# One tile step of a macaron transformer kernel: reordered output path, one 17-column power, one sine product per q or k

## The reference, cut to what matters

```python
for l in range(2):                              # the stack, run twice in the kernel
    q, k, v = split(shift_token(x) @ wqkv[l])   # 8 heads of 64
    q, k = l2norm(q) * q_scale, l2norm(k) * k_scale
    q, k = rotary_xpos(q, k)                    # q * cos * s + rotate_half(q) * sin * s, k with 1 / s
    o = local_attention(q * 8, k, v)            # window 64, looks one window back
    x = x + o @ wo
    h = layernorm(shift_token(x)) * g + b
    a, g = split(h @ w1 + b1)
    x = x + (a * gelu(g)) @ w2 + b2
```

## Time and profile before

| | |
|---|---|
| median of 3 runs | 1783.23 us (1782.45 to 1784.5) |
| the profiled execution | 1786.46 us, its span 1784.7 us |
| PE busy | 1515.6 us, 85% |
| DVE busy | 1358.0 us, 76% |
| ACT busy | 1139.9 us, 64% |
| POOL busy | 1095.8 us, 61% |
| mean granted TensorE clock | 0.969 of full speed |

### The profile page before, as it was taken

One profiled execution on the slowest core, in us unless ns is written; L12 is line 12 of the kernel. 1 busy time (PEld: TensorE's weight loads), 2 busy tenths in 40 slices (PEclk: granted clock), 3 DMA queues, 4 the chain that ended last, 5 costly groups with the idle time before them and its releaser, 6 DMA issues.

```text
span 1784.7 us, 44020 instructions
## 1 busy us (share of the span) xinstructions
PE 1515.6 (85%) x15864; PEld 1233.3 (69%) x15864; DVE 1358.0 (76%) x3516; ACT 1139.9 (64%) x2364; POOL 1095.8 (61%) x1106
## 2 busy tenths in 40 slices
PE   1789999978999899977888889989998889999974
PEld 1577777766777777755666667777776777777763
DVE  6687878768787978767776479787977687979772
ACT  1576767667686767634455467676766576767671
POOL 3676868577585858623333278585857485858560
PEclk9899999989999999988999999999999999999996
DMA  8231212132221222113100132121223221212113
GB/s 284 50 122 43 57 41 62 48 95 50 68 51 48 51 71 51 40 29 122 36 25 21 46 96 54 45 54 45 63 57 87 59 60 44 54 44 54 45 28 119
DMA packets 183670, 112.46 MB, mean 63 GB/s; under 512 B 86720, under 2 KB 164128, under 8 KB 182944
## 3 DMA queue, kind: packets, MB, share of 16 engines
q1 hardware_dynamic: 183456, 109.65, 23.5%
HBM read 43.41 MB, written 23.42 MB: 37 GB/s over the span
## 4 chain that ended last, share of the span: by engine, by line
PE 50%; DVE 26%; ACT 9%; issue 7%; SPq 3%; DMA 2%; POOL 1%; DVEq 0%; ACTq 0%; POOLq 0%
PE QK L389 9%; PE TO L639 8%; PE QK L639 5%; PE TO L706 5%; DVE rope_c L1154 5%; DVE rope_s L1159 4%; DVE o_n L1179 4%; DVE top L1098 3%; PE SC L680 3%; ACT probs L1303 3%; PE TO L389 3%; PE TO L752 3%; DVE h2n L1166 3%; PE TO L808 2%; PE VB L808 2%
## 5 line engine op out<-in xcount | busy, mean ns | idle before, releaser
L1303 ACT ACTIVATE probs<-SC,shift,qgain 128x128 f32<-128x128 f32 x1024 | 390.6, 481 | 101.9 <-DVE shift L1106 101.6
L1481 POOL TENSOR_TENSOR ve<-mv,epsilon 128x1 f32<-128x1 f32 x128 | 24.5, 192 | 392.8 <-DVE mv L1145 392.8
L389 PE MATMUL QK<-w_qkv,hT 128*128 128x512 f32 x768 | 220.7, 424 | 25.5 <-DMA w_qkv<-qkv_d 12.0
L1154 DVE TENSOR_TENSOR rope_c<-QK,rope 128x512 f32<-128x512 f32 x256 | 175.7, 686 | 80.5 <-PE QK L389 78.1
L1494 POOL TENSOR_TENSOR rnorm<-clip,mhalf 128x8 f32<-128x8 f32 x128 | 211.1, 1649 | 12.4 <-DVE clip L1115 12.2
L1503 POOL TENSOR_TENSOR qgain<-clip,mhalf 128x8 f32<-128x8 f32 x128 | 209.5, 1637 | 0.0
L639 PE MATMUL TO<-ident,probs 128*128 128x128 f32 x1280 | 189.9, 276 | 12.0 <-ACT probs L1303 11.1
L1098 DVE TENSOR_REDUCE top<-SC 128x4 f32<-128x512 f32 x256 | 174.8, 683 | 31.1 <-PE SC L680 30.9
L1297 ACT ACTIVATE v_own<-VB 128x512 f32<-128x512 f32 x128 | 76.5, 598 | 189.2 <-PE VB L389 189.2
L1159 DVE TENSOR_TENSOR rope_s<-QK,rope 128x256 f32<-128x256 f32 x512 | 191.0, 415 | 0.0
L639 PEld LDWEIGHTS TO<-ident,probs 128*128 128x128 f32 x1280 | 153.8, 142 | 45.0 <-issue 24.8
(11 more groups left out here) (174 smaller groups left out, 3745.0 us busy)
## 6 DMA issues: line engine op xcount, KB each, us to landing
v_prev<-v_own SPq DMA_DIRECT2D x256, 130.0 KB, 2.3
x_att<-stream SPq DMA_DIRECT2D x128, 64.0 KB, 2.2
h<-stream SPq DMA_DIRECT2D x256, 32.0 KB, 1.9
stream<-x_new SPq DMA_DIRECT2D x32, 256.0 KB
w_qkv<-qkv_d SPq DMA_DIRECT2D x3, 1536.0 KB, 7.5
h<-x_mid SPq DMA_DIRECT2D x128, 32.0 KB
h<-x_mid SPq DMA_DIRECT2D x128, 31.8 KB
rope<-rope_d SPq DMA_DIRECT2D x24, 128.0 KB, 3.2
```

The costliest lines, as they stand in the source:

```text
L389: last = mm(dst, fr(left(a)), fr(right(b)), start=(k == 0), stop=(k == 2))
L1154: v.tensor_tensor(qk(rope_c[:])[:, m], src, rope[:, i, m, 0:1, :].to_broadcast([P, HEADS, DH]), ALU.mult)
L1303: last = nc.scalar.activation(probs[:, b, hd, :], SC[:, hd * P:hd * P + P], ACT.Exp, bias=shift[:, b, hd:hd + 1], scale=qgain[:, b, hd % 4 ...
```

## The change

- PE transposes `o_n` one step later, as part of WO's stage (WO's tile is ATT's of the step before), right behind the q and k transposes. The v product goes ahead of the q and k products. WO's product follows them; both halves of the probabilities are transposed after it.
- ACT copies oT right behind kT and qT, and then takes all eight exponentials of ATT's tile in one run. In a step after a burst they were already taken at the end of the burst step.
- POOL takes one power a step over 17 columns (8 of q, 8 of k, 1 variance), first in its step, then `k_r`, `x_b2`, `q_r`, `k_a`. The separate addition of epsilon and two powers go. The scale of 8 moves into the rope table.
- DVE clips 16 columns in one operation, adds epsilon itself (one column, written beside them), and makes the sine product of q or k in one operation of 512 columns that reads the halves in reversed order. The low parts come ahead of the second maxima; the sum of squares is last, in a burst step it lies inside the burst.
- In the burst the PSUM banks are swapped (`banks`), and the second W2 half goes to TT.

```diff
@@ PE step
-                    if t := tile(ATT):
-                        probs_transposed(t, 0)
                     if t := tile(WO):
-                        ... (wait s_oT, s_xn; WO product into OB)
+                        pe.wait_ge(s_on, t.count())
+                        for c in range(PAIRS):
+                            last = transpose(OB[:, c * P:c * P + P], o_n[:, c * P:c * P + P])
+                        last.then_inc(s_to, 1)
                     if t := tile(QKV):
                         pe.wait_ge(s_hl, t.count())
+                        if t2 := tile(FFN_IN + 1):
+                            pe.wait_ge(s_h2l, t2.count())
+                        product(mm, VB[:], ... w_qkv[:, x, 1024:1536]).then_inc(s_v, 1)
...
                             product(mm, QK[:, m * 512:m * 512 + 512], ...).then_inc(signal, 1)
-                        product(mm, VB[:], ... w_qkv[:, x, 1024:1536]).then_inc(s_v, 1)
+                    if t := tile(WO):
+                        pe.wait_ge(s_oT, t.count())
+                        for c in range(PAIRS):
+                            last = mm(OB[:, 0:DIM], oT[:, c, :], w_o[:, c, :], ...)
+                        last.then_inc(s_y, 1)
+                    if t := tile(ATT):
+                        probs_transposed(t, 0)
                     if t := tile(ATT):
                         probs_transposed(t, 1)
...
-                    if t := tile(ATT):
-                        pe.wait_ge(s_on, t.count())
-                        ... (the o_n transposes)
@@ DVE step
-                if t := tile(QKV + 1):
-                    clipped(t)
                 if t := tile(FFN_IN):
                     v.bn_stats(st2[:, b, :], h2[:, k, :]).then_inc(s_st2, 1)
+                if t := tile(QKV + 1):
+                    clipped(t)
+                if t := tile(FFN_IN):
+                    dve.wait_ge(s_st2, t.count())
+                    v.bn_aggr(mv2[:, t.i % 2, :], st2[:, t.i % 2, :]).then_inc(s_mv2, 1)
+                    dve.wait_ge(s_mv2, t.count())
+                    v.tensor_scalar(squares[:, t.i % 4, 16:17], mv2[:, t.i % 2, 1:2], EPS, None, ALU.add).then_inc(s_ve2, 1)
...
-                        for half in range(2):
-                            a, o = 32 * half, 32 * (1 - half)
-                            last = v.tensor_tensor(qk(rope_s[:])[:, m, :, a:a + 32], src[:, :, o:o + 32], ...)
+                        last = v.tensor_tensor(qk(rope_s[:])[:, m].rearrange("p h (a d) -> p h a d", a=2),
+                                               src.rearrange("p h (a d) -> p h a d", a=2)[:, :, ::-1, :],
+                                               sin.to_broadcast([P, HEADS, 2, 32]), ALU.mult)
...
-                    dve.wait_ge(s_rs2, t.count())
+                    dve.wait_ge(s_pw, t.powers(FFN_IN))
...
+                if t := tile(TQK):
+                    highest(t, 1)
+                    shifted(t, 1)
+                if burst is None and (t := tile(QKV)):
+                    squares_summed(t)
@@ ACT step
+                if t := tile(WO):
+                    act.wait_ge(s_to, t.count())
+                    copy(oT[:], OB[:]...).then_inc(s_oT, 1)
+                if before is None and (t := tile(ATT)):
+                    exponentials(t, 0)
                     exponentials(t, 1)
@@ POOL step
+                t, t2 = tile(QKV + 1), tile(FFN_IN)
+                if t:
+                    pool.wait_ge(s_cl, t.count())
+                if t2:
+                    pool.wait_ge(s_ve2, t2.count())
+                if t or t2:
+                    k, cols = (t or t2).i % 4, slice(0 if t else 16, 17 if t2 else 16)
+                    g.tensor_tensor(inverse[:, k, cols], squares[:, k, cols], mhalf[:, cols], ALU.pow).then_inc(s_pw, 1)
+                if t := tile(QKV + 1):
+                    pool.wait_ge(s_pw, t.powers(QKV + 1))
+                    g.tensor_tensor(k_r ..., k_a ..., inverse[:, t.i % 4, 8:16] ..., ALU.mult).then_inc(s_kr, 1)
                 if t := tile(FFN_IN):
-                    ... (ve2, rstd2)
                     pool.wait_ge(s_xm, t.count())
                     g.tensor_tensor(x_b2[:, i, :], x_mid[:, i, :], b_2[:], ALU.add).then_inc(s_xb2, 1)
-                if t := tile(QKV + 1):
-                    ... (rnorm, k_r, qgain)
```

More of the change, by code:

```diff
@@ L64, in count, with powers @@
         return ((self.c - back + self.first) // every + 1) * unit
+    def powers(self, skew):
+        return self.c + (skew - QKV) + self.first // NT * (NT + FFN_IN - QKV - 1)
     def loads(self):
@@ L169, in build @@
         norm2 = sb("norm2", [P, 2, 2 * HEADS])
-        clip2 = sb("clip2", [P, 2, 2 * HEADS])
-        rnorm = sb("rnorm", [P, 2, HEADS])
-        qgain = sb("qgain", [P, 2, HEADS])
+        squares = sb("squares", [P, 4, 2 * HEADS + 1])
+        inverse = sb("inverse", [P, 4, 2 * HEADS + 1])
         rope_c = sb("rope_c", [P, 2 * INNER])
@@ L275, in build @@
         s_ve2 = sem("s_ve2")
-        s_rs2 = sem("s_rs2")
         s_h2n = sem("s_h2n")
@@ L713, in f @@
                         pe.wait_ge(s_hl, t.count())
+                        if t2 := tile(FFN_IN + 1):
+                            pe.wait_ge(s_h2l, t2.count())
+                        if before is not None:
+                            pe.wait_ge(s_xn, before * 2 + 1)
+                        product(mm, VB[:], lambda x: hT[:, b, x, :], lambda x: w_qkv[:, x, 1024:1536]).then_inc(s_v, 1)
                         if t2 := tile(TQK):
@@ L798, in w2_half @@
                 def w2_half(half):
-                    dst = VB if half == 0 else OB
+                    dst = VB if half == 0 else TT
                     pe.wait_ge(s_act2, n * 6 + (3 * half + 3))
@@ L1106, in shifted, with squares_summed @@
                 v.scalar_tensor_tensor(out=shift[:, t.i % 2, hd], in0=top[:, t.i % 2, hd], scalar=-1.0,
-                                       in1=qgain[:, t.i % 2, :].rearrange("p (c e) -> p e c", e=2)[:, half], op0=ALU.mult, op1=ALU.mult).then_inc(s_sh, 1)
+                                       in1=inverse[:, t.i % 4, 0:8].rearrange("p (c e) -> p e c", e=2)[:, half], op0=ALU.mult, op1=ALU.mult).then_inc(s_sh, 1)
+            def squares_summed(t):
+                b = t.i % 2
+                dve.wait_ge(s_sq, t.count())
+                v.tensor_reduce(norm2[:, b, :], sq[:].rearrange("p (h d) -> p h d", d=DH), AX, ALU.add).then_inc(s_n2, 1)
             def clipped(t):
-                b = t.i % 2
+                k = t.i % 4
                 dve.wait_ge(s_n2, t.count())
[L1113 to L1116, removed]
+                if t.c >= 4:
+                    dve.wait_ge(s_pw, Tile(t.c - 4, t.first // NT).powers(QKV + 1))
+                v.tensor_scalar(squares[:, k, 0:16], norm2[:, t.i % 2, :], 1e-24, None, ALU.max).then_inc(s_cl, 1)
             def step(tile, burst, before):
@@ L1360, in step @@
                                              bias=b_1[0:m, 3 + c:4 + c]).then_inc(s_gelu, 1)
+                    if t := tile(TQK):
+                        need(act, s_tp, t.count(back=2, unit=2))
+                        exponentials(t, 0)
+                        exponentials(t, 1)
             act.wait_ge(s_w, N_CONST)
@@ L1484, in step @@
+                if t := tile(FFN_IN):
+                    i = t.i
                     if i == 0:
                         pool.wait_ge(s_ffnw, t.loads() * 96 - 15)
-                        k = t.count(back=TILES, every=TILES, unit=2)
-                        need(pool, s_xn, k)
+                        n = t.count(back=TILES, every=TILES, unit=2)
+                        need(pool, s_xn, n)
                     pool.wait_ge(s_xm, t.count())
                     g.tensor_tensor(x_b2[:, i, :], x_mid[:, i, :], b_2[:], ALU.add).then_inc(s_xb2, 1)
-                if t := tile(QKV + 1):
[L1492 to L1503, removed]
```

85 lines of the change are left out of this document (28 added, 57 removed).

## The result

| | before | after |
|---|---|---|
| median of 4 runs | 1783.87 us | 1827.14 us |
| ratio to before | 1 | 1.0243, 95% interval 1.0226 to 1.0259 |
| span of the profiled execution | 1784.7 us | 1826.0 us |
| a regular step | 9.19 us | 9.87 us |
| a burst and the step behind it | 23.97 + 9.47 us | 23.47 + 8.80 us |

The changed kernel is 2.4% slower. (This "before" has one more run than the table ahead of the prediction.) The step lengths are distances between the starts of h2n: the middle one of 101 (before) and 105 (after) for a regular step; the pair of after is that of most pairs; of the 14 pairs before, six are as shown, five are 0.3 us shorter (23.66 + 9.47) and three are longer (34.2 to 36.7 us), two of them with a wait for weights.

The account below looks back on a forecast made before the run. Taken as the bound: the products' loop of DVE and PE now, the loop through GpSimd's power after. On the 1783.2 us median, +54 us for regular steps and -16 for bursts, in total +38, gave 1821 us; range 1742 to 1847.

Parts of the forecast that it names:

- The loop: Regular step after: power, h2n, maxima, shift, o_n, low parts, maxima, squares, statistics, epsilon, power; 9.80 us against 9.19.
- the held shift: DVE's first shift, due at 1.84 us behind the power, is held by GpSimd's q_r to 2.79.
- the release of the power: GpSimd starts the power 0.08 us after DVE's addition of epsilon ends, at 6.75 us in the step.
- The power's price: GpSimd: one column takes 0.56 us, eight 1.65, so 17 columns take 0.40 + 17 x 0.156 = 3.05 us.
- its bounds of 2.35 to 3.4: 17-column power: 2.35 us with nine further columns at half price, 3.4 as two of eight with 0.1 for the last.
- The sum: 88 regular steps add 54 us, 14 bursts with the step behind gain 1.15 us each (-16); in total +38 us.
- The shift is not held: Rival: q_r starts after the first shift is due, so a regular step takes 8.95 us; 1738 us in all, chance 0.25.
- The power is cheaper: Rival: the 17-column power takes 2.5 us or less, a regular step 9.26; 1773 us in all, chance 0.10.
- dearer: Rival: power of 3.4 us or sine product of 0.9 adds 0.2 to 0.35 a step; 1840 to 1850, chance 0.10.
- 0.5 us of cover: Loop of PE products, x_mid and rope to h2n: about 0.5 us to spare a step, as h2n is held anyway.

Follow-up runs that it names:

- experiments 6: The changed kernel with the v product moved behind the q and k products and WO; 1824.85 us, ratio 1.0232.
- 7: The changed kernel with one more power, of a single column, issued on GpSimd ahead of the 17-column one; 1879.62 us, ratio 1.0544.
- experiment 1: The changed kernel with the first shift of a step issued behind o_n instead of ahead of it; 1750.69 us, ratio 0.9813.
- experiments 4: The changed kernel with the sine product of q or k again in two halves of 256 columns; 1829.57 us, ratio 1.0254.
- experiment 5: The kernel before with the one-piece sine product alone; 1773.07 us, ratio 0.9939.
- experiment 3: The changed kernel with one wait added, so that GpSimd starts k_r only when h2n is done; 1801.54 us, ratio 1.0097.
- experiments 2: The changed kernel with the 17-column power cut into 9 columns ahead of k_r and 8 behind it; 1723.96 us, ratio 0.9662.
- 8: The changed kernel with two powers (9 columns, then 8 behind k_r) and q_r waiting for the second shift; 1715.6 us, ratio 0.9625.

## Why the prediction was right

**The loop.** The steps of the working, put at K = 0 at the end of the power (606.73), stand beside the trace of after: k_r at 0.08 (predicted 0.08), the first maxima at 1.13 (1.13), q_r at 1.50 (1.50), the shift due at 1.84 (1.84) and held to 2.79 (2.79), o_n at 3.02 (3.02), the low part at 3.63 (3.63), the squares at 4.82 (4.82), the statistics at 5.95 (5.95). All of it came from pitches of one step and one meeting. That the loop is the power's is what experiments 6 and 7 show, that the held shift is in it experiment 1. The first shift takes 0.9 to 1.0 us in 101 of the 128 tiles, so the step shown is the rule.

**The one term that was mis-sized** is the release of the power. Predicted start 6.75, measured 6.80: the addition of epsilon ends at 613.36, and GpSimd starts 0.17 us later, not 0.08. The power took 3.07 instead of 3.05. With the addition 0.03 us earlier than predicted, these make 9.87 of 9.80.

**The power's price** came from two points, one and eight columns, 0.40 + 0.156 a column. Nine columns gave 1.80 (1.80) and seventeen 3.07 (3.05). A line through two points was right here; its bounds of 2.35 to 3.4 were needed only because no third point stood in the trace.

**Two things were argued wrongly and did no harm to the number.** The first is about the kernel before: "GpSimd isn't on it: between its power of rnorm and the use of it there is room." There is none. The power ends at 370.92 and k_r starts at 371.00, and the held h2n passes k_r's end on to the maxima. In that kernel the regular steps whose h2n is held take 9.19 us (the middle one of 52), those whose h2n is free 9.11 (of 25). A hold is counted as busy time of the engine that is held, so the chain of waits, with GpSimd at 1%, doesn't show it. The forecast took the 9.19 us from the trace, so it didn't depend on this.

The second is about the kernel after. I said that the output transposes have their input a whole step early. They don't: TensorE waits 1.12 us for o_n there, and TensorE's chain of o_n, output transposes, v, q and k, WO and x_mid runs through them. TensorE, after, as against the earlier trace rows:

```profile
610.49 0.66 PE L638 MATMUL TO<-ident,o_n 128*128 128x128 f32 x4 [1.12 <-DVE o_n L1182]
610.98 0.94 PE L388 MATMUL VB<-w_qkv,hT 128*128 128x512 f32 x3
611.75 1.56 PE L388 MATMUL QK<-w_qkv,hT 128*128 128x512 f32 x6
613.15 1.05 PE L728 MATMUL TO<-w_o,oT 128*128 128x128 f32 x8
```

I had v wait for the low parts, 0.06 us past their end, and the transposes behind o_n end at nearly the same moment, so x_mid came at 7.51 (predicted 7.49).

**The sum.** By the starts of h2n, the two stacks' regular steps up to tile 59 (90 of them, where I had 88) went from 849.0 to 904.9 us, +55.9 (predicted +54). The 14 pairs of a burst and the step behind it went from 472.2 to 452.7, -19.5 (predicted -16); 9.0 of the 19.5 come from the three that were longest before; in two of them GpSimd's `x_b` waits for a weight load, 3.1 and 3.2 us. Draining the second stack took 4.7 us longer (27.5 to 32.2), and the rest 0.2. The whole is +41.3 on the span, +43.3 on the medians, against +38. That the parts agree this closely is luck in part. Eighty of the regular steps grew by 0.76 us each on average, more than the predicted 0.61, since the step grew by 0.07 more and many of them had taken 9.11 and not 9.19 before; ten that were long before (9.6 to 17.2 us) gave 4.7 us back. The 11 other pairs gained 10.5 us instead of 11 x 1.15 = 12.7, since the pair that the forecast was read from was of the longer kind, and the three longest made up for it.

**The rivals.** "The shift is not held" is refuted by the row at 608.57, and priced by experiment 1: with the shift free the kernel takes 1751 us, where I gave that case 1738. "The power is cheaper" and "dearer" are refuted by the 3.07 us; the reversed read costs what a straight one does, 0.68 us and a pitch of 0.60. A one-piece sine product and v ahead of q and k were costed at nothing, with 0.5 us of cover; experiments 4 and 6 bear that out, and experiment 5 shows what the first is worth without the cover.

## What to carry to other kernels

A short operation of VectorE like the shift here, with both inputs in SBUF, can cost a loop not its own 0.16 us but the rest of whatever GpSimd is streaming: lay both timelines side by side and look at what stands beside it after the change. Merging operations saves the engine's time and may lengthen the path: one power of 17 columns frees GpSimd, but it delays the first user by the columns that this user doesn't need. When a change moves the bound to another loop, its savings elsewhere become worth nothing until that loop is mended; here two powers instead of one turned 2.4% slower into 3.4% faster. And look at all the meetings before moving one: what experiment 3 gained at h2n it lost again at the second shift.

## What the runs showed of the hardware

- A held VectorE operation is served when the running GpSimd stream ends, even if the next stream follows without a gap: with the shift held to 609.52, k_a started at 609.45, at its usual pitch of 1.22 behind q_r. In the ten traces 1798 shifts and h2n took over 0.4 us. Every one of them ends 0.01 to 0.09 us behind the end of the stream that ran when it was issued or began within 0.08 us (k_r, q_r, k_a, or x_b with its 128 columns); the longest takes 1.30 us, so none was held by two streams.
- A GpSimd power doesn't hold a shift that meets it (0.16 us at 546.85, beside the power of 546.09 to 547.73), while streams of 512 columns do. In the kernel before and in experiments 2 and 8, 322 shifts run wholly inside a power, and none takes over 0.17 us. The Trainium skill, "SBUF — State Buffer", "Who interferes with whom", makes no such difference: there any GpSimd instruction that reads SBUF holds the ports for its whole length. Here the measurement decides.
- Who comes first is not decided by the start alone when the two are close. In the kernel before, h2n is held in all 79 steps in which it starts 0.01 to 0.08 us ahead of k_r (1.13 to 1.21 us), and takes 0.34 us in the 30 in which it is 0.13 us or more ahead, up to 0.55.
- Reading PSUM with the two halves of each head in reversed order costs the same as reading it straight: 681 ns in the mean for both products of 512 columns.
- GpSimd starts 0.17 us after the end of the VectorE addition that releases it (613.36 to 613.53), and 0.08 us after the end of its own power. The 0.17 is not a price for every release by VectorE: before, the addition of epsilon on GpSimd started at 368.06, 0.08 us behind the moments (367.81 + 0.17).
